# GpSimd's clears ahead of the second layer's 71 result stores are taken out

## The reference

```
x = x + L0_ffn(L0_cond(fside, cond, x, coeffs), ...)      # 8 gelu experts, top 2, gated sum
x = x + L1_ffn(L1_cond(x, cond, Wx, Wh, b), ...)          # tanh recurrence over 128 steps, then:
   w   = top-2 softmax gates of layernorm(h) @ gate_w.T
   out = swiglu(h, shared weights)
   for e in range(8):
       out = out + w[:, e:e+1] * (silu(h @ Wg[e]) * (h @ Wu[e])) @ Wd[e]
```

## Time and profile before

| | us |
|---|---|
| median of three runs | 484.55 |
| profiled execution | 485.34 |
| its span | 483.5 |
| TensorE matmul busy | 406.6 (84%) |
| VectorE busy | 338.7 (70%) |
| GpSimd busy | 329.3 (68%) |
| of it result stores L553, x142, mean 969 ns | 137.6 |
| of it clears L509, x151, median 325 ns | 49.1 |
| ScalarE busy | 206.4 (43%) |

### The profile page before, as it was taken

The page is one execution under the profiler, slowest core; times in us unless marked ns, Lnnn a source line. Parts: engine busy times, 40 slices in busy tenths (PEclk is TensorE's granted clock), DMA queues, the critical chain, the costliest instruction groups (busy, mean ns, idle before and its releaser), DMA issues.

```text
span 483.5 us, 10308 instructions
## 1 busy us (share of the span) xinstructions
PE 406.6 (84%) x2428; PEld 332.5 (69%) x2428; DVE 338.7 (70%) x1299; ACT 206.4 (43%) x660; POOL 329.3 (68%) x440
## 2 busy tenths in 40 slices
PE   3878985558999999999999999988968999997420
PEld 3465654535999999767788977765757888886320
DVE  4788687287888888866677577787696777774462
ACT  1221112213777777645545255434333555554110
POOL 0558888888877777773466456658467888788880
PEclk9898567575999999999998599999898999999585
DMA  5994111116454432633211111125122533321845
GB/s 151 287 340 141 39 44 41 45 41 144 102 140 115 110 104 78 192 133 107 61 40 41 34 34 39 35 60 120 44 56 79 130 89 89 85 78 41 290 140 184
DMA packets 48151, 49.79 MB, mean 103 GB/s; under 512 B 8627, under 2 KB 37246, under 8 KB 47966
## 3 DMA queue, kind: packets, MB, share of 16 engines
q1 hardware_dynamic: 38680, 30.46, 23.9%
q0 software_dynamic: 8640, 17.84, 11.1%
q10 hardware_dynamic: 774, 0.84, 0.6%
HBM read 27.99 MB, written 21.12 MB: 102 GB/s over the span
## 4 chain that ended last, share of the span: by engine, by line
PE 60%; DVE 13%; POOL 13%; issue 7%; DMA 4%; ACT 1%; SPq 1%; DVEq 0%; POOLq 0%; ACTq 0%
PE banks L1272 50%; POOL regions L519 8%; PE banks L1276 8%; POOL pause L509 3%; PE banks L1361 3%; DMA parts<-results 2%; POOL results L553 1%; DMA results<-y_row,y_dest 1%; DVE y_row L1054 1%; DMA base<-in_x 1%; DVE state_lo L1145 1%; DVE act_row L1152 1%; DMA regions<-parts,pos 0%; ACT wgu_hi L618 0%; DVE base L1204 0%
## 5 line engine op out<-in xcount | busy, mean ns | idle before, releaser
L553 POOL DMA_INDIRECT results<-y_row,y_dest x142 | 137.6, 969 | 51.2 <-DVE y_row L1054 20.8
L519 POOL DMA_INDIRECT regions<-first_w,pos x64 | 62.3, 973 | 51.4 <-ACT hT L655 33.4
L519 POOL DMA_INDIRECT regions<-parts,pos x64 | 64.0, 1000 | 18.0 <-POOL pause L509 18.0
L655 ACT ACTIVATE hT<-banks,pcol 128x32 f32<-128x32 f32 x128 | 36.8, 287 | 58.6 <-PE banks L1272 58.0
L714 ACT ACTIVATE silu_row<-banks 128x256 f32<-128x256 f32 x75 | 28.8, 383 | 76.7 <-PE banks L1272 76.7
L637 ACT COPY act_col<-banks 128x256 f32<-128x256 f32 x146 | 54.0, 370 | 11.3 <-PE banks L1276 10.3
L1272 PEld LDWEIGHTS banks<-hT,wh 128*128 128x128 f32 x256 | 42.3, 199 | 22.8 <-ACT hT L655 18.3
L1276 PE MATMUL banks<-const_sb,act_row 128*128 128x128 f32 x292 | 57.2, 278 | 0.0
L1276 PEld LDWEIGHTS banks<-const_sb,act_row 128*128 128x128 f32 x292 | 42.2, 145 | 19.4 <-issue 2.3
L1152 DVE TENSOR_TENSOR act_row<-silu_row,banks 128x256 f32<-128x256 f32 x75 | 31.4, 420 | 32.0 <-ACT silu_row L714 29.8
L509 POOL MEMSET pause<- 128x256 f32 x151 | 49.1, 325 | 5.6 <-issue 5.4
(11 more groups left out here) (192 smaller groups left out, 861.8 us busy)
## 6 DMA issues: line engine op xcount, KB each, us to landing
parts<-results SPq DMA_DIRECT2D x16, 512.0 KB, 4.9
hT<-regions SPq DMA_DIRECT2D x71, 65.0 KB
wgu<-regions SPq DMA_DIRECT2D x71, 65.0 KB
results<-y_row,y_dest POOLq DMA_INDIRECT x142, 2.3
base<-in_x SPq DMA_DIRECT2D x12, 128.0 KB, 3.0
out<-base SPq DMA_DIRECT2D x20, 64.0 KB
regions<-const_sb SPq DMA_DIRECT2D x18, 65.0 KB
first_w<-in_L_ffn_W SPq DMA_DIRECT2D x1, 1024.0 KB, 7.9
```

The lines of the kernel that those rows point to most:

```text
L519: pool.indirect_dma_start(regions[layer], bass.IndirectOffsetOnAxis(ap=poss[layer][q][:, t, k:k + 1], axis=0), hrows[layer][:, q, t, k, :] ...
L553: pool.indirect_dma_start(results[layer], bass.IndirectOffsetOnAxis(ap=y_dest[:, s:s + 1], axis=0), y_row[:, s, :], None).then_inc(results ...
L655: nc.scalar.activation(hT[:, hcols(n, step_col(s), B)], rnn_ps[:, p, step_col(s):step_col(s) + B], ACT.Tanh, bias=pcol[:, ROW_CB:ROW_CB + ...
```

## The change

More of the change, by code:

```diff
@@ L576, in _ @@
                         scatter1(SPLIT * NT * TOPK + i)
-                rest()
                 send_result(1, r)
```

## The result

The changed kernel took 465.27 us, the median of four runs (464.02, 464.10, 466.45, 469.34), against 483.58 us of four runs before. The ratio is 0.9644, 95% interval 0.9567 to 0.9720. So it is faster: by 18.3 us between these medians, and by 17.2 us as the ratio has it, with an interval of 13.5 to 20.9 that still holds the 14.6 forecast. But 465.27 lies 1.2 us under the range (466.5 to 474.5). The profiled execution took 464.02 us around a span of 462.2.

A forecast was written before the change was run, and what follows sets the result against it. The prediction took GpSimd's queue of stores and clears, not TensorE, as the bound: 15.1 us gained at the last store less 0.5 in the tail, 14.6 off the median 484.55, gives 470.0 us; range 466.5 to 474.5.

The forecast's parts named there:

- A bare store's interval: GpSimd's second-layer result stores without clears: 1.265 us apart instead of 1.567, so 0.30 us saved per removed clear.
- Catching up: GpSimd, storing faster than VectorE's 1.484 us a slot, meets its results at slot 47, four slots later with a long gap.
- Slot 54's store: The store that the first load of `parts` waits for: starts at 433.0 instead of 445.88.
- The stall gone: VectorE's 9.7 us wait for the first load of `parts` vanishes, 3.2 us to spare; its 1.4 us additions cost 0.
- The last store: Slot 70's result store starts at 456.5 instead of 471.62, gaining 15.1 us, with 0.5 us included for long operations.
- The tail: From last store's start to the end: the 11.9 us stay, plus 0.5 us because ScalarE's outputs now lie directly ahead.
- The sum: Whole kernel: 15.1 us from the last store less 0.5 for the tail, 14.6 us off.
- no late terms: Range's lower bound, 466.5 us: none of the small added delays occurs, and a run is as low as 480.97.
- A (interval does not hold): Rival: second-layer stores come 1.45 us apart because neighbouring work differs, VectorE stands 2.2 us; 475 us, chance 0.07.
- B (tail swells): Rival: last stores, outputs and loads crowd together, the last store landing in 6.2 us; 474 us, chance 0.08.
- C (bare stores slow VectorE): Rival: stores press on VectorE through the shared interface; 0.45 us more in slots 16 to 70 gives 495 us, chance 0.03.
- D (nothing): Rival: something the clear only hid keeps GpSimd's store interval; 484.5 us, chance 0.03.

The follow-up runs named there:

- runs 3 and 4: Against the kernel before: VectorE's additions moved later, all clears kept, ratio 1.0005; clears removed only ahead of slots 55-70 (0.9893), 0-15 (0.9935) or 0-54 (0.9702).
- the repeats: The changed kernel measured twice more without any edit: medians 470.02 and 468.51 us, ratios 0.9677 and 0.956 to the kernel before.
- after_again: The changed kernel measured again without any edit: 470.02 us, ratio 0.9677 to the kernel before.
- before_again: The kernel before, measured again without any edit for a second trace: 483.82 us.
- bare_first16: The kernel before with clears removed only ahead of the second layer's result stores of slots 0 to 15: 479.77 us, ratio 0.9935.
- sums_late: The kernel before, all clears kept, VectorE's additions of blocks 0 to 2 moved behind slots 68, 69 and 70: 481.98 us, ratio 1.0005.
- short_clear: The kernel before with the 71 clears ahead of the second layer's result stores cut from 128x256 to 128x1: 469.05 us, ratio 0.9725.

## Why the prediction was right or wrong, point by point

**What bounds the kernel** was right: GpSimd's queue sets the last store, and the engine is neither the busiest one nor the one that leads the chain. The account by dates kept it from counting the stall's 9.7 us as a gain of their own; runs 3 and 4 show that this would have been wrong.

**A bare store's interval**, 1.265 us: measured 1.263 (375.87 to 377.13 and on), or (26.8 + 9.5) / 28 = 1.296 over the stretch from 376 to 412 with its one long gap:

```profile
L553 POOL DMA_INDIRECT results<-y_row,y_dest x28 | 26.8, 957 | 9.5 <-issue 5.8 <-DVE y_row L1053 3.7
```

**Catching up** at slot 47, or four later with a long gap: it was slot 45, gap included. That is two errors that met, not a good count. Slot 16's store was put 7.9 us behind its result's start and stood 6.6 behind it: slot 9's store, said to stay, started 0.62 us behind its result's start instead of 1.10, and the results of slots 9 to 16 took 12.3 us, not 11.5. The date is not in the sum as long as it lies ahead of slot 54. **Slot 54's store** 57.6 us behind slot 16's result: it took 426.89 - 369.31 = 57.6. **The stall gone**: right, and TensorE did not wait at the two additions of 1.4 us behind slot 61.

**The last store** 81.1 us behind slot 16's result: 80.9, and 80.7 and 80.4 in the repeats. The three long stores came to 1.1 us in all over 0.96 each, every one beside an addition of two SBUF tensors (at 437.09, 440.39 and 444.55). But behind the first of them GpSimd waited 0.78 us for slot 62's result, so its 0.45 cost nothing; the other two moved the last store by 0.66 us, where 0.5 were taken. The results came a little sooner than forecast, which made up for it. By the rule of the Trainium skill ("GPSIMD Engine Reference", section 1, Specifications), that GpSimd contends with VectorE's instructions with two SBUF inputs, such stores are expected; the trace agrees in kind, with 1.1 us in all and 0.66 that counted, against the 3.7 that every addition would have made.

**The tail** was put at 12.4 us, 0.5 over before, for outputs and loads that crowd together. It took 12.0, 11.8 and 11.7, on average 0.1 under the 11.9 of before. This term, 0.5 in the sum, was wrong; the outputs went by without delaying the loads (2.8 and 5.0 us, as before).

**The sum**: 14.6 us forecast. From slot 16's result to the end the three traces of the changed kernel took 92.9, 92.5 and 92.1 us, mean 92.5, the two of before 108.1 each: 15.6. The mechanism held and the size was 1.0 us short: 0.6 of it is the tail, and 0.4 the last store (15.1 forecast, 15.5 measured).

**What failed is the step from the sum to the range**, "no late terms, and a run as low as the 480.97 among the three". It took the three runs before as the whole spread, and put at nothing how far an execution moves ahead of slot 16: slot 16's result came between 368.9 and 378.4 us in ten traces with the same work ahead of it, clears aside. The bound does not even follow from its own words: with no late terms the sum is 15.6 off, and 480.97 - 15.6 = 465.4, not 466.5; the measured 465.27 would lie 0.1 under that too. And the forecast subtracted from a median, 484.55, that was 1.3 us above the mean of all 53 runs, 483.2. 483.2 - 15.6 = 467.6 would have been the forecast with both known, and the 17 runs of the changed kernel average 467.4. The four that decided were 464.0 to 469.3, their median 2.1 under that average.

So of the 18.3 us measured, 15.6 are shown in the traces as the change. The other 2.7 are put down to chance in two small samples. That is argued, not shown: the means of all runs, 15.8 apart, agree, while the runs that the ratios keep are 17.1 apart, so a further 1 or 2 us of real gain are not ruled out.

**The rivals**: A (interval does not hold) no: 1.263. B (tail swells) no: the tail is as long as before. C (bare stores slow VectorE) no: the slot took (436.11 - 369.31) / 45 = 1.484 us, as before to the last digit. D (nothing) no.

**What stays open** is what sets off the low clock in the recurrence, and whether anything of the gain lies outside the stretch from slot 16's result to the end.

## What to carry to other kernels

A queue that runs behind its producer is costed by its throughput: count the instructions from the point where it falls behind to the last one, times the interval, and stop counting where it catches up; a stall elsewhere that hangs on the same queue is a second sight of the same cost and is not added. Look at what each date depends on before adding waits out of a chain. And where only three runs are given, take the place in the trace that the change can't reach, ask how far it moves from one execution to the next, and widen the range by that: here slot 16's result moved over 9.5 us in single traces, and the medians of the changed kernel lay between 465.3 and 470.0, so 3 us to either side is a fair estimate for a median of four.

## What the runs showed of the hardware that was not expected

TensorE's granted clock falls while it is fully busy and nothing in these columns announces it. The kernel before, in stretches of 4 us; the columns are those above:

```profile
260.00:264.00 4.00, 4.00 (x24) 3.19 (x23) 3.25 (x17) 2.87 (x8) 2.62 (x4) 0.88 0.12 38
264.00:268.00 4.00, 4.00 (x17) 3.64 (x16) 2.19 (x9) 0.86 (x3) 3.20 (x3) 0.50 0.12 36
...
272.00:276.00 4.00, 4.00 (x16) 3.64 (x17) 2.57 (x13) 0.98 (x4) 0.97 (x2) 0.50 0.05 17
276.00:280.00 4.00, 4.00 (x29) 3.67 (x29) 0.82 (x4) 1.43 (x5) 2.21 (x2) 0.91 0.05 17
280.00:284.00 4.00, 4.00 (x26) 2.92 (x24) 3.53 (x16) 2.47 (x8) 2.34 (x3) 1.00 0.10 33
```

PE was busy all through, the clock went from 1.00 to 0.50 (1.2 GHz) by 264 us, stayed there to 276 and came back. In after_again the same happened at 280, in another stretch:

```profile
276.00:280.00 4.00, 4.00 (x26) 3.24 (x24) 2.69 (x16) 2.93 (x9) 2.52 (x4) 0.94 0.10 33
280.00:284.00 4.00, 4.00 (x16) 3.55 (x16) 2.31 (x7) 0.90 (x4) 3.47 (x4) 0.50 0.15 50
284.00:288.00 4.00, 4.00 (x16) 3.64 (x15) 2.65 (x15) 1.74 (x5) 2.29 (x3) 0.50 0.10 33
...
292.00:296.00 4.00, 4.00 (x30) 3.28 (x29) 1.81 (x11) 2.40 (x7) 1.50 (x2) 1.00 0.10 33
```

The first trace of the changed kernel, before_again and bare_first16 have no such episode from 240 to 300 us, and in them slot 16's result came at 369; in the six traces with one it came between 374.0 and 378.4. In sums_late it came at 373.0 without one there; it entered the recurrence 1.7 us later than before_again and lost the rest in pieces of about 1 us. From the last result of the first layer to the first of the second the six with an episode took 133.3 to 135.4 us and the four without 129.4 to 130.9, so an episode costs some 3 to 6 us, mostly 5.

A store of GpSimd and an addition of VectorE with two SBUF inputs hold each other up, and by an amount that can be read off. In the changed kernel's trace:

```profile
440.39 0.68 DVE L1203 TENSOR_TENSOR base<-base,parts 128x512 f32<-128x512 f32 x1
```

```profile
444.55 0.69 DVE L1204 TENSOR_TENSOR base<-base,parts 128x512 f32<-128x512 f32 x1
...
447.61 0.75 DVE L1204 TENSOR_TENSOR base<-base,parts 128x512 f32<-128x512 f32 x1
```

```profile
447.64 0.96 POOL L553 DMA_INDIRECT results<-y_row,y_dest  x1 [0.31 <-issue]
```

The stores that start 0.12, 0.27 and 0.18 us behind an addition's start are 0.45, 0.28 and 0.38 us longer than 0.96: they end as if they had begun some 0.57 us into the addition. This holds for all 34 stores beside these additions, in the twelve traces of this study, that start 0.06 to 0.49 us into one (start and excess add up to between 0.55 and 0.57 each time). Those that start 0.56 us or more into one are not longer, nor are those that begin ahead of it, and an addition that begins while a store is under way keeps its usual 0.68 or 0.69 us. And where the two start within 0.04 us of each other, nine times, the store keeps its 0.96 us and the addition takes 0.74 to 0.76 instead of 0.69, as at 447.61. So a long store costs at most some 0.5 us, and only where it falls into the first half microsecond.

And what a wait of GpSimd for its own memset costs depends on what else it waits for. In arrears it costs nothing that can be seen: the gap ahead of a store is 0.28 us behind such a wait and 0.30 us without one. Where GpSimd stands waiting for a result, it does cost. Slot 1's result and store, before and then in the changed kernel:

```profile
342.48 0.34 DVE L1054 TENSOR_SCALAR y_row<-banks,wgu 128x128 f32<-128x128 f32 x1
```

```profile
343.59 0.96 POOL L553 DMA_INDIRECT results<-y_row,y_dest  x1 [1.16 <-DVE y_row L1054]
```

```profile
337.71 0.34 DVE L1053 TENSOR_SCALAR y_row<-banks,wgu 128x128 f32<-128x128 f32 x1
```

```profile
338.32 0.96 POOL L553 DMA_INDIRECT results<-y_row,y_dest  x1 [1.65 <-DVE y_row L1053]
```

The store starts 1.11 us behind its result's start with a clear ahead and 0.61 without, though the memset had ended before the result began; in short_clear, with the small memset, it is 1.12. From slot 12 on, where a store also waits for the one 12 before it, it is 1.10 us without a clear too (slots 45 to 61). That points to a second wait ahead of the store as the cost, whatever it waits for; no run here varies it by itself.
